# Masked cross attention in a decoder: two float32r parts with two heads in a tile, in place of three bfloat16 parts, and the preparation of a batch moved earlier

## The reference

```
q = (Wq @ x + bq) * mask          # 256 x 512, likewise k of the context
v = Wv @ context + bv
scores[h] = q[h].T @ k[h] / 4 + mask terms of +-1e6       # 512 x 512 for each of 16 heads
out = softmax(scores) @ v, times mask;   x = layernorm(x + out)
```

## Time and profile before

| | us |
|---|---|
| median of three runs | 3795.46 |
| lowest and highest | 3790.32, 3798.69 |
| profiled execution, its own time | 3798.53 |
| its span | 3796.7 |
| mean granted TensorE clock | 0.925 |
| first and last exponential matmul (L1341) of the stage begin at | 539.6, 1281.7 |

### The profile page before, as it was taken

The page is one execution under the profiler, slowest core; times in us unless marked ns, Lnnn a source line. Parts: engine busy times, 40 slices in busy tenths (PEclk is TensorE's granted clock), DMA queues, the critical chain, the costliest instruction groups (busy, mean ns, idle before and its releaser), DMA issues. The chain is left out here.

```text
span 3796.7 us, 48928 instructions
## 1 busy us (share of the span) xinstructions
PE 3083.9 (81%) x16338; PEld 2017.6 (53%) x16339; DVE 1707.7 (45%) x3299; ACT 1276.3 (34%) x3252; POOL 579.1 (15%) x581
## 2 busy tenths in 40 slices
PE   6999656666667469999978888599999997799894
PEld 5666412222222156777665555488888886444441
DVE  5666634454555322111215666366666664211113
ACT  2333224444445311111104444355565553111110
POOL 1000111111111120000000000233333332300002
PEclk9999868888888779999988999799999998999997
DMA  1000145554544220000010000211121113500323
GB/s 67 12 22 22 37 75 87 93 91 91 92 84 79 80 78 23 12 12 12 12 47 12 22 22 17 100 40 45 48 81 62 45 34 115 225 0 33 122 87 109
DMA packets 141460, 222.98 MB, mean 59 GB/s; under 512 B 14696, under 2 KB 66376, under 8 KB 141296
## 3 DMA queue, kind: packets, MB, share of 16 engines
q1 hardware_dynamic: 124736, 182.35, 19.0%
q0 software_dynamic: 7664, 27.40, 2.1%
q10 hardware_dynamic: 8896, 11.07, 1.0%
HBM read 157.36 MB, written 58.82 MB: 57 GB/s over the span
## 5 line engine op out<-in xcount | busy, mean ns | idle before, releaser
L1255 DVE TENSOR_REDUCE x_minus_max<-banks 128x2 f32<-128x1024 f32 x256 | 308.9, 1221 | 375.9 <-PE banks L1323 371.3
L1194 ACT ACTIVATE x_probs<-banks 128x512 f32<-128x512 f32 x512 | 293.0, 596 | 337.6 <-PE banks L1341 255.6
L1341 PE MATMUL banks<-x_stacked_q,x_stacked_k 105*128 105x512 bf16 x512 | 210.2, 417 | 107.5 <-DMA x_stacked_q<-x_max_rows 60.0
L1323 PE MATMUL banks<-x_stacked_k,x_stacked_q 102*128 102x512 bf16 x512 | 173.2, 424 | 117.4 <-DMA x_stacked_k<-x_mask_parts_dram 115.6
L481 ACT ACTIVATE a_probs<-banks,a_minus_max 128x128 f32<-128x128 f32 (+1 forms) x512 | 209.0, 426 | 145.4 <-DVE a_minus_max L564 143.5
L1341 PEld LDWEIGHTS banks<-x_stacked_q,x_stacked_k 105*128 105x128 bf16 x512 | 50.2, 100 | 333.4 <-ACT x_probs L1194 188.7
L2073 POOL TENSOR_TENSOR x_probs<-x_probs,x_inverse 128x512 f32<-128x512 f32 x128 | 133.3, 1042 | 274.5 <-DVE x_inverse L2282 274.5
L2137 ACT ACTIVATE x_probs<-banks,x_minus_max,x_rroot 128x256 f32<-128x256 f32 x256 | 143.1, 566 | 91.3 <-DVE x_minus_max L2248 91.3
L2807 DVE TENSOR_TENSOR m_h<-banks,m_silu 128x512 f32<-128x512 f32 x39 | 27.0, 692 | 318.5 <-PE banks L2923 165.3
L564 DVE TENSOR_REDUCE a_minus_max<-banks 128x2 f32<-128x512 f32 (+1 forms) x192 | 131.9, 687 | 82.1 <-PE banks L714 61.6
L1645 DVE TENSOR_TENSOR f_hT<-banks,f_silu 128x256 f32<-128x256 f32 (+1 forms) x88 | 37.3, 424 | 281.2 <-ACT f_silu L1571 281.2
(11 more groups left out here) (373 smaller groups left out, 7749.9 us busy)
## 6 DMA issues: line engine op xcount, KB each, us to landing
x_x<-x_after SPq DMA_DIRECT2D x24, 512.0 KB, 4.3
x_parts_dram<-x_parts SPq DMA_DIRECT2D x16, 768.0 KB, 9.2
x_stacked_q<-x_parts_dram SPq DMA_DIRECT2D x48, 256.0 KB
x_stacked_k<-x_parts_dram SPq DMA_DIRECT2D x48, 256.0 KB
x_after<-a_z SPq DMA_DIRECT2D x16, 512.0 KB, 2.8
x_z<-x_after SPq DMA_DIRECT2D x16, 512.0 KB, 3.8
x_after<-x_z SPq DMA_DIRECT2D x16, 512.0 KB, 3.1
x_context<-in_ctxT SPq DMA_DIRECT2D x16, 512.0 KB, 5.5
```

Of the source, the lines that this page charges most:

```text
L1194: act.activation(probs[:, n % 8, :], psum[at.bank(f"exp{n}")], ACT.Exp, scale=SCALE)\
L1255: dve.tensor_reduce(minus_max[:, c % 2, h % 4, 2 * (n % 2):2 * (n % 2) + 2], at.pair(use), AX.X, ALU.max, negate=True)\
L1323: ins = pe.matmul(at.pair(use)[:, k, :], stacked[0][to][0:MAX_ROW, h, t * P:(t + 1) * P], stacked[1][to][0:MAX_ROW, h, :], start=True, sto ...
L1341: ins = pe.matmul(psum[at.bank(use)], stacked[1][u][:, h, s * P:(s + 1) * P], stacked[0][u][:, h, :], start=True, stop=True)
```

## The change

Only the masked cross attention changes.

- Two float32r parts instead of three bfloat16 parts: one rounding (ACT), one subtraction (POOL). Three products instead of six, so a head takes 3 x 16 + 3 mask + 2 maximum rows = 53 rows; an even head stands on rows 0 to 52 and an odd one on rows 64 to 116 of the same tile. `score` step n now takes one tile of positions for two heads, one matmul on each half. A stack is now, for each of k and q, 2 x (3 copies of 16 rows, 1 copy of 3 mask rows), all of float32.
- `project+`, `finish+`, `whole+`, `round+` work two batches ahead (slots 24, 28, 40, 44), a piece in two steps, and `write_parts` at the end of SP's list. `stack` then is at the head of SP's list of the batch after, behind the heads of the last context and ahead of the sums; `load_inputs` for the batch after next moves up too, behind `z`.
- Scores run 14 pairs ahead instead of 11 (the next batch's begin at slot 36), maxima and shifts are at slots 4 and 7 (and 16, 32, 48 later) instead of 9 and 11, the values at 9 and 14, `inverse''` at 15 instead of 9, `inverse` at 48, both `stats` later. A shift is two DMAs instead of three.
- A lead-in of two sequences instead of one: the parts of batch 0, then those of batch 1 with the scores of batch 0.

```diff
 ROWS = MAX_ROW + PARTS
 SCALE = float(CH) ** -0.5
 NEG = 1e6
-UNIT_LEAD = 22
+UNIT_LEAD = 28
 UNITS_IN_TAIL = 1
-MAXIMA_AT = 9
-SHIFT_AT = 11
+MAXIMA_AT = 4
+SHIFT_AT = 7
 SLOTS = 4 * 16
-PIECES_AT = (1, 5, 9, 13)
-VALUES_AT = (31, 37)
+PIECES_AT = (24, 28, 40, 44)
+VALUES_AT = (9, 14)
 FOLD = 32
-
-
-def xattn_schedule(has_prev, own, has_next):
+HALF = 64
+STACKED_PAIRS = ((0, 0), (0, 1), (1, 0))
+STACKED_MASK = 48
+STACKED_MAX = 51
+STACKED_ROWS = 53
...
+def xattn_schedule(has_prev, own, has_next, has_second):
...
+        there = {"''": has_prev, "'": has_next, "+": has_second}
...
     for q in range(SLOTS + 4):
@@ -828,11 +839,11 @@
             if q % 2 == 0 and q >= 2 * UNITS_IN_TAIL:
                 add(("score", n) if n < 32 else ("score'", n - 32))
         for n, start in enumerate(PIECES_AT):
-            for kind, at in (("project'", 0), ("whole'", 2), ("round'", 3), ("again'", 6)):
+            for kind, at in (("project+", 0), ("finish+", 1), ("whole+", 3), ("round+", 4)):
                 if q == start + at:
                     add((kind, n))
         for n, start in enumerate(VALUES_AT):
-            for kind, at in (("values'", 0), ("bias'", 2), ("mask'", 3)):
+            for kind, at in (("values'", 0), ("more'", 1), ("bias'", 3), ("mask'", 4)):
                 if q == start + at:
                     add((kind, n))
         for kind, at in (("maxima", MAXIMA_AT), ("shift", SHIFT_AT)):
@@ -840,7 +851,7 @@
                 add((kind, (q - at) // 16 + 1))
             if q == at + 48:
                 add((kind + "'", 0))
-        for step, at in ((("inverse''", 1), 9), (("stats''", 1), 28), (("normalise''", 0), 34), (("inverse", 0), 43), (("stats", 0), 58)):
+        for step, at in ((("stats''", 0), 4), (("inverse''", 1), 15), (("stats''", 1), 36), (("normalise''", 0), 42), (("inverse", 0), 48)):
             if q == at:
                 add(step)
         for n in range(UNITS_IN_TAIL):
@@ -872,19 +883,20 @@
                 ring[0] += 1
             elif kind == "exp":
                 out.append((f"{tag}exp{n}", 4 + n % 2))
-            elif kind in ("shift", "shift'", "project'", "values'"):
+            elif kind in ("shift", "shift'", "project+", "values'"):
                 out.append((f"{tag}{kind}{n}", 7))
             elif kind == "context" and n % 4 == 0:
                 out.append((f"{tag}context{n // 4}", 6))
...
-            def stack(w, b, u):
-
-
-                sp.wait_ge(third_part, b * 4 + (w + 1) * 2)
-                sp.dma_start(parts_dram[w, u].rearrange("k (c p) s -> p k c s", p=P), parts[:, w]).then_inc(parts_written, 16)
-                sp.wait_ge(parts_written, (b * 2 + (w + 1)) * 16)
-                for j, pair in enumerate(PAIRS):
-                    sp.dma_start(stacked[w][u][CH * j:CH * (j + 1)], parts_dram[w, u, pair[w]].rearrange("(h d) s -> d h s", d=CH))\
-                        .then_inc(stacked_ready[w][u], 16)
-                if w == 1:
-                    sp.wait_ge(cleared, 2)
-                sp.dma_start(stacked[w][u][MASK_ROW:MAX_ROW],
-                             mask_dram[w, b].unsqueeze(1).broadcast_to([len(PAIRS), H, POS])).then_inc(stacked_ready[w][u], 16)
+            def write_parts(b, u):
+
+                for w in range(2):
+                    sp.wait_ge(low_ready, b * 4 + (w + 1) * 2)
+                    sp.dma_start(parts_dram[w, u].rearrange("k (c p) s -> p k c s", p=P), parts[:, w]).then_inc(parts_written, 16)
+
+            def stack(b, u):
+
+
+                sp.wait_ge(parts_written, b * 32 + 32)
+                for w in (1, 0):
+                    for half in range(2):
+                        for j, pair in enumerate(STACKED_PAIRS):
+                            sp.dma_start(stacked[w][u][HALF * half + CH * j:HALF * half + CH * (j + 1)],
+                                         parts_dram[w, u, pair[w]].rearrange("(h g d) s -> g d h s", g=2, d=CH)[half])\
+                                .then_inc(stacked_ready[w][u], 16)
+                        sp.dma_start(stacked[w][u][HALF * half + STACKED_MASK:HALF * half + STACKED_MAX],
+                                     mask_dram[w, b].unsqueeze(1).broadcast_to([len(STACKED_PAIRS), H // 2, POS]))\
+                            .then_inc(stacked_ready[w][u], 16)
...
             def run(steps, at, b, u):
-                prev, own, following = ("stats''", 1) in steps, ("exp", 0) in steps, ("project'", 0) in steps
-                if not prev and not own:
-                    sp.wait_ge(mask_written, 16 * 2 * len(PAIRS))
+                prev, own = ("stats''", 1) in steps, ("exp", 0) in steps
+                following, second = ("values'", 0) in steps, ("project+", 0) in steps
+                if following and not own:
+                    sp.wait_ge(mask_written, 16 * 2 * len(STACKED_PAIRS))
+                    sp.wait_ge(cleared, 4)
                 if prev:
                     move_heads(b - 1, 1 - u, 3)
+                if following:
+                    stack(b + 1, 1 - u)
+                if prev:
                     fold_sums(b - 1, 1 - u, 1)
                 if own:
                     if not (isinstance(b, int) and b < 2):
                         sp.wait_ge(stored[u], at.in_turn * 16)
                     load_rows(b, u)
+                if own and second:
+                    sp.wait_ge(v_ready, b * 2 + 2)
+                    load_inputs(b + 2, u)
                 if prev:
                     spread_inverse(b - 1, 1 - u, 1)
                 if own:
                     move_heads(b, u, 0)
-                if following:
-                    for w in range(2):
-                        stack(w, b + 1, 1 - u)
-                if own:
                     move_heads(b, u, 1)
                     fold_sums(b, u, 0)
                 if prev:
                     store(b - 1, 1 - u)
-                if own and not (isinstance(b, int) and b + 2 >= B):
-                    sp.wait_ge(v_ready, b * 2 + 2)
-                    load_inputs(b + 2, u)
                 if own:
                     spread_inverse(b, u, 0)
                     move_heads(b, u, 2)
+                if second:
+                    write_parts(b + 2, u)
...
-                        for k in range(PARTS):
-                            act.dma_start(stacked[0][to][MAX_ROW + k:MAX_ROW + k + 1, 4 * n:4 * n + 4, :],
-                                          max_rows[4 * k:4 * k + 4, n % 2, :]).then_inc(shift_ready[n % 2], 16)
-                    if kind == "round'":
+                        for half in range(2):
+                            row = HALF * half + STACKED_MAX
+                            act.dma_start(stacked[0][to][row:row + 2, 2 * n:2 * n + 2, :],
+                                          max_rows[4 * half:4 * half + 4, n % 2, :]).then_inc(shift_ready[n % 2], 16)
+                    if kind == "round+":
                         w, m = n // 2, n % 2
-                        act.wait_ge(whole_ready, (b + 1) * 4 + (n + 1))
-                        act.copy(parts[:, w, 0, m, :], whole[:, w, m, :]).then_inc(first_part, 1)
-                    if kind == "again'":
-                        w, m = n // 2, n % 2
-                        act.wait_ge(rest_ready, (b + 1) * 4 + (n + 1))
-                        act.copy(parts[:, w, 1, m, :], rest[:, w, m, :]).then_inc(second_part, 1)
+                        act.wait_ge(whole_ready, (b + 2) * 4 + (n + 1))
+                        high_part_act(act, parts[:, w, 0, m, :], whole[:, w, m, :]).then_inc(high_ready, 1)
...
-                        for k in range(2):
-                            t = 2 * (n % 2) + k
-                            ins = pe.matmul(at.pair(use)[:, k, :], stacked[0][to][0:MAX_ROW, h, t * P:(t + 1) * P],
-                                            stacked[1][to][0:MAX_ROW, h, :], start=True, stop=True)
+                                pe.wait_ge(stacked_ready[w][to], at.loads(ahead) * 8 * 16)
+                        for half in range(2):
+                            rows = slice(HALF * half, HALF * half + STACKED_MAX)
+                            ins = pe.matmul(at.pair(use)[:, half, :], stacked[0][to][rows, h, t * P:(t + 1) * P].bitcast(F32R),
+                                            stacked[1][to][rows, h, :].bitcast(F32R), start=True, stop=True)
...
-                            pe.wait_ge(shift_ready[c % 2], (b * 2 + (c // 2 + 1)) * PARTS * 16)
-                        ins = pe.matmul(psum[at.bank(use)], stacked[1][u][:, h, s * P:(s + 1) * P], stacked[0][u][:, h, :], start=True, stop=True)
+                            pe.wait_ge(shift_ready[c % 2], (b * 2 + (c // 2 + 1)) * 32)
+                        rows = slice(HALF * (h % 2), HALF * (h % 2) + STACKED_ROWS)
+                        ins = pe.matmul(psum[at.bank(use)], stacked[1][u][rows, h // 2, s * P:(s + 1) * P].bitcast(F32R),
+                                        stacked[0][u][rows, h // 2, :].bitcast(F32R), start=True, stop=True)
...
```

(33 more changed lines are left out.)

133 lines of the change are left out of this document (61 added, 72 removed).

## The result

The changed kernel takes 3807.07 us (median of 6, 3803.1 to 3815.96) where the kernel before takes 3795.48 (6 runs, 3790.32 to 3798.69): ratio 1.0035, interval 1.0021 to 1.0048. It is slower by 0.35%, clear of the interval; the forecast was 3716 with a range of 3635 to 3780. The profiled execution took 3803.1 us, span 3801.3.

What follows compares the result with a forecast made beforehand. TensorE was taken to wait for stack copies and shift rows in masked cross attention, 98.5 us a batch. Savings of 49 + 14 + 14 + 2 = 79, and 3.1 for the median, off 3798.5 gave 3716; range 3635 to 3780.

Steps and rivals of the forecast that it cites:

- Step 1: Stack copies: 3.34 MB a batch still onto 16 rows at 119 GB/s, 28.1 us, bounds 10.3 to 35.3.
- Step 2: SP's queue: stacks issued first end at 33.4 us, scores never wait; sums, then inputs land behind, slot 24 at 42.
- The wait at inverse'': DVE at slot 15 waits over 10 us for sums landing at about 35.5, putting slot 20 at 37.
- The stop of 16 us at project+: TensorE at slot 24 waits for inputs until 42 instead of 26; 10 us or more would show the forecast right.
- Step 3: Other 40 slots: 36.8 us, less 1.2 for shifts, plus 9.6 projection and 1.5 clock; batch 88.7 instead of 98.5.
- Step 4: The slots' own rate under the new matmuls: no change taken, bounds -1.6 and +3 us a batch.
- the bound of 3: Upper bound on slower slots: +3 us a batch, 0.2 us a group for weight loads.
- Step 5: DVE, POOL and ACT savings stay hidden; the shift may cost 4 us at slot 16, within Step 2's stop.
- Step 6: Stage ends: first exponential near 545 instead of 539.6; batch 0 gains 14 us, batch 6 14, batch 7 2.
- A: Rival, fast stacks: larger pieces move at 163 GB/s, 3665 us, or at 323, some 3615; chance 0.23.
- B: Rival, little gain: stacks at the upper bound, first exponential held 15 us for stack 1, 3774 us; chance 0.14.
- C: Rival, slower matmuls: 188 ns weight loads no longer hidden on 51 or 53 rows, 144 us, 3860; chance 0.11.

Runs made afterwards that it cites:

- full_rows: The changed kernel with every score and exponential matmul over all 128 rows, scale cut, output different: 3780.4 us, ratio 0.9964.
- si_zero_start: sums_inputs_first with exact 128-row matmuls, zeros in added rows, later second stats and normalise, first zero fills before VectorE's first wait: 3663.2 us, ratio 0.9659.
- si_stats_late: sums_inputs_first, half rows, with the previous batch's second stats at slot 44 instead of 36 and normalise at 50 instead of 42: 3680.8 us, ratio 0.9716.
- si_full_rows: sums_inputs_first with score and exponential matmuls over all 128 rows, scale cut, output different: 3689.7 us, ratio 0.9742.
- si_rows72: sums_inputs_first with score and exponential matmuls over rows 0 to 71 for either head, scale cut, output different: 3744.3 us, ratio 0.9880.
- sums_inputs_first: The changed kernel with the sums and the inputs of project+ both issued ahead of the stack on SP's queue: 3711.5 us, ratio 0.9789.
- si_scale: sums_inputs_first with only the exponential's scale cut by 1e-9, so every probability is 1, as a control: 3708.7 us, ratio 0.9785.

## Why the prediction was wrong

**Step 1, the stacks: right.** From 632.93 on they moved at 122 to 131 GB/s in windows of 5 us until 660, where the rate rose to 193: about 28 us, as forecast.

**Step 2, the queue: one half right, and its order of landing wrong.** The wait at inverse'' was foreseen, and that the stacks no longer stop the scores. The stop of 16 us at project+, a sign of being right, never came: the sums held TensorE until 670.1, and when it reached project+ at 677.2 the context was there. Counted from 627.6, where the forecast's stack at 5.3 matches the 632.93, the sums were due at 35.5 and came at 40.4; TensorE was to go on at 37 and did at 42.5; project+ was due at 42 and came at 49.6. The step took the queue to deliver in the order of issue, the sums right behind the stack and the inputs behind those. Instead z and x, issued behind the sums, landed 4.2 and 0.9 us before them, and context 4.7 us after. The Trainium skill (DMA: Bandwidth & Descriptors, Two DMAs through the same engine are not ordered) says that the descriptors in one queue of one engine start in order but are pipelined, and that nothing orders copies across the 16 engines. These landings agree. The forecast also had TensorE reach project+ within 5 us of going on; it had stood a slot or two further back, and took 7.1. Slots 7 to 23 were to take 34.7 and took 40.1: 27 us in five batches.

**Step 3, the other slots: mis-sized, by the clock.** 54 us were forecast for slots 23 to 7, with 1.5 for the clock. They took 61.5, 37 us in five batches. The same slots take some 53 at the full clock, so the count of work was right and all of the 37 goes with the clock. In full_rows, which pays for its serial pairs, they take 57.6: that got back 20 of the 37.

**Step 4, "I take nothing": the step that failed in kind.** It asked whether a matmul takes longer, and at full clock the slots do not: context steps in the last batch still follow each other by 3.2 us in places, near the 3.11 of the earlier trace rows. It did not ask what a matmul over half the rows does to the clock that is granted afterwards. It was to stay as in the earlier trace rows; it fell by 0.1 in five batches and by 0.25 in the last. The price, some 8 us a batch (61.5 against 53), is above the bound of 3. What full rows get back of it, 27 us in full_rows against the change and 22 in si_zero_start against si_stats_late, is less, since their pairs run one behind the other.

The step also left out the turning from half rows to 128 and back. At full clock an exponential between two pieces of the values, first in the changed kernel, then in si_full_rows:

```profile
644.33 1.13 PE L1373 MATMUL banks<-x_w_v,x_context 128*128 128x256 f32 x4
645.39 0.49 PE L1343 MATMUL banks<-x_stacked_q,x_stacked_k 53*128 53x512 f32 x1
645.81 1.13 PE L1373 MATMUL banks<-x_w_v,x_context 128*128 128x256 f32 x4
```

```profile
641.36 1.02 PE L1374 MATMUL banks<-x_w_v,x_context 128*128 128x256 f32 x4
642.03 0.59 PE L1344 MATMUL banks<-x_stacked_q,x_stacked_k 128*128 128x512 f32 x1
642.46 1.03 PE L1374 MATMUL banks<-x_w_v,x_context 128*128 128x256 f32 x4
```

The pieces start 1.48 us apart over half rows and 1.10 over 128, 0.38 more for one turn and back. Sixteen such visits a batch (projections, values, shifts) would be 6 us of TensorE's time, an estimate from these rows; how much of it the stage pays was not measured, but at full clock its slots are no slower for it.

**Step 5:** hidden engines stayed hidden. The shift at slot 16 still cost a wait of 2.9 to 5.6 us, but outside the stop of step 2, not within it: first one, then the other, in the rows of TensorE above.

**Step 6, the ends:** scores began at 514.8 and the exponentials at 542.6 (forecast 517 and 545). Slot 7 of batch 1 came 8 us late all the same (636.3; 545 + 77 + 6.4 is 628.4), for batch 0 already ran at a clock of 0.80. Batch 6 took 83.2 us for 79.5. The last one took 59.7 from slot 7 to the last copy of a context (1227.17 to 1286.84) where some 50 were implied (1284.31 less slot 7 of that batch, less the 2 of the step); its clock was 0.72.

**Sum.** 8 + 64 + 4 + 10 = 86 of the 91 us between 3716 and 3807. The others are offsets: the forecast took 3.1 off for the median and 3 less for batch 0 than its own numbers gave, the profiled run lies 4 below its median, and 2 us came behind the stage. Of the 86, 27 lie in the slots of step 2's stop, and most of the rest goes with the clock (step 4). Removing both waits of step 2 gained more than 27, 93 us, since the forecast had kept a stop of 16 us a batch.

**The rivals.** A is out. B had little gain, 21 us, but for another reason (stacks at an upper bound). C named the right side and the right instructions, but its mechanism is not what decided: not the weight loads, and not the turning between modes. The drain at a change of mode that the Trainium skill (TensorEngine Tiling (Array Packing), Key Properties) names can be seen, about 0.2 us each way in the rows under step 4; but si_rows72 has no half-array mode and is the slowest of its group. At 144 us C was also priced at more than twice what went with the clock. The order in the queue, which decided, stood inside the forecast's own step 2 with its bound on the wrong quantity: the rate of the stacks was bounded, not the landing of what lay behind them.

## What to carry to other kernels

When a large copy is moved ahead on a queue, list everything that is issued in its shadow, before or after, and count on all of it landing near the last byte; then put whatever an engine waits for soon ahead of it, all of it at once, since removing one of two waits that end together shows nothing. When packing matmuls into fewer rows, look at the granted clock of the stretch before and after: here, where TensorE had idle time, fuller rows were worth more than the overlap, even with zeros in the added rows. An experiment that shows nothing after taking one wait away has not cleared that wait.

## What the runs showed of the hardware

The granted clock fell to the lower level (1.2 of 2.4 GHz) in stretches where TensorE never stood still for 1 us. In the changed kernel:

```profile
790.00:794.00 4.00, 3.13 (x17) 1.11 (x16) 3.56 (x4) 3.28 (x7) 0.00 (x0) 1.00 0.00 1
794.00:804.00 10.00, 10.00 (x32) 3.27 (x35) 4.89 (x10) 4.28 (x8) 3.17 (x3) 0.58 0.08 18
```

Between 788.4 and the fall, near 796, there are only slots of 51 and 53 rows and context steps, with pauses of 0.5 to 0.8 us. With the same schedule over 128 rows the clock of the whole span is 0.942 instead of 0.916 (si_full_rows and sums_inputs_first), over 72 rows 0.912; with zeros in the added rows it is 0.944 instead of 0.928 (si_zero_start and si_stats_late). So in these kernels the rows that a matmul covers count for the grant, zeros too; the data of the probabilities did not (si_scale). Why, no run shows, and half-row kernels with fewer stops were granted more as well (0.81 to 0.87 from the first to the last exponential).

A copy of 16 KB, issued behind 3.3 MB, landed 27.7 us later, about with 2 MB that were issued behind it. And float32r matmuls on two halves of the rows run side by side. A score pair at full clock, over half rows in the changed kernel, then over 128 rows in si_full_rows:

```profile
641.35 0.41 PE L1325 MATMUL banks<-x_stacked_k,x_stacked_q 51*128 51x512 f32 x2
```

```profile
701.22 0.62 PE L1326 MATMUL banks<-x_stacked_k,x_stacked_q 128*128 128x512 f32 x2
```

One matmul alone takes 0.39 to 0.50, so the half-row pair takes no longer than one. Where an exponential comes first on one of the halves, the pair's records span 0.72, since one of the two waits for it.
